# A fused feed-forward, attention, feed-forward block: new rope, projections, root mean square and order of units in the attention stage

## The reference

```
x = x + 0.5 * ffn(layernorm(x))        # mixture of 8 experts, 2 chosen
x = x + attention(layernorm(x))
x = x + 0.5 * ffn(layernorm(x))
```

```
q, k, v = x Wq^T + bq, x Wk^T + bk, x Wv^T + bv
q1, q2, k1, k2 = rope(each)                    # (x1 cos - x2 sin, x1 sin + x2 cos)
a1, a2 = softmax(causal(q1 k1^T / sqrt 8)), softmax(causal(q2 k2^T / sqrt 8))
out = (a1 - lam a2) v                          # lam per head, from lq1, lk1, lq2, lk2
out = out * rsqrt(mean(out*out over 8) + 1e-6) * head_norm_w * 0.8
result = out Wo^T + bo
```

## Time and profile before

| | |
|---|---|
| median of three runs | 1861.6 us |
| profiled execution | 1863.29 us |
| its span, first to last instruction | 1861.6 us |
| mean granted TensorE clock | 0.968 of full speed |
| PE busy | 1608.8 us, 86% |
| DVE busy | 1363.2 us, 73% |
| ACT busy | 1269.4 us, 68% |
| POOL busy | 1046.3 us, 56% |

### The profile page before, as it was taken

The page is one execution under the profiler, slowest core; times in us unless marked ns, Lnnn a source line. Parts: engine busy times, 40 slices in busy tenths (PEclk is TensorE's granted clock), DMA queues, the critical chain, the costliest instruction groups (busy, mean ns, idle before and its releaser), DMA issues. The chain is left out here.

```text
span 1861.6 us, 43161 instructions
## 1 busy us (share of the span) xinstructions
PE 1608.8 (86%) x16448; PEld 1220.1 (66%) x16448; DVE 1363.2 (73%) x3442; ACT 1269.4 (68%) x1613; POOL 1046.3 (56%) x707
## 2 busy tenths in 40 slices
PE   4999999994588888888888888888873799999998
PEld 3787777883466666666666666666652577778787
DVE  5777777765778778878887788788742677777775
ACT  4777777772167767767677677677664577777776
POOL 4888888875324434334344343343312688888885
PEclk9999999997699999999999999999996799999999
DMA  3333323321323233232232332322302232233331
GB/s 113 103 114 115 102 88 108 109 103 46 87 79 92 58 91 82 66 94 72 76 94 61 86 87 60 95 78 70 89 12 77 97 115 90 93 114 110 108 109 63
DMA packets 142846, 163.14 MB, mean 88 GB/s; under 512 B 13244, under 2 KB 124558, under 8 KB 141454
## 3 DMA queue, kind: packets, MB, share of 16 engines
q1 hardware_dynamic: 142640, 160.38, 28.8%
HBM read 91.20 MB, written 14.70 MB: 57 GB/s over the span
## 5 line engine op out<-in xcount | busy, mean ns | idle before, releaser
L292 POOL TENSOR_TENSOR ffn_h_low<-ffn_h,ffn_h_high 128x1024 fp32r<-128x1024 f32 x192 | 458.4, 2401 | 95.0 <-ACT ffn_h_high L341 94.8
L1019 ACT ACTIVATE att_prob<-att_ring 128x1024 f32<-128x1024 f32 x384 | 388.6, 1022 | 155.9 <-PE att_ring L1240 153.4
L1125 DVE TENSOR_REDUCE att_nmax<-att_ring 128x4 f32<-128x1024 f32 (+1 forms) x384 | 450.8, 1217 | 54.3 <-PE att_ring L1240 54.3
L479 DVE TENSOR_TENSOR ffn_h<-ffn_up,ffn_comb_wide 128x1024 f32<-128x1024 f32 x256 | 311.3, 1216 | 125.1 <-ACT ffn_up L334 122.8
L334 ACT ACTIVATE ffn_up<-ffn_up 128x1024 f32<-128x1024 f32 x256 | 258.1, 1008 | 202.8 <-PE ffn_up L567 201.1
L341 ACT ACTIVATE ffn_h_high<-ffn_h 128x1024 fp32r<-128x1024 f32 x256 | 269.3, 1052 | 0.7 <-DVE ffn_h L479 0.7
L935 POOL TENSOR_TENSOR att_qk<-att_turned 128x512 f32<-128x512 f32 x64 | 81.4, 1273 | 318.0 <-DVE att_turned L1104 318.0
L1240 PE MATMUL att_ring<-att_qs,att_kd 64*128 64x256 bf16 (+1 forms) x2048 | 151.1, 249 | 95.4 <-DVE att_nmax L1125 57.2
L567 PE MATMUL ffn_up<-ffn_xt_high,ffn_w_high 128*128 128x512 f32 x512 | 214.7, 419 | 1.7 <-DVE ffn_h L479 1.6
L580 PE MATMUL ffn_y<-ffn_h_high,ffn_w_high 128*128 128x512 f32 x512 | 205.3, 401 | 7.0 <-POOL ffn_h_low L292 6.0
L284 POOL TENSOR_TENSOR ffn_ez<-ffn_e_const,ffn_nz 128x16 f32<-128x16 f32 x64 | 185.6, 2901 | 38.2 <-DVE ffn_nz L405 38.2
(11 more groups left out here) (146 smaller groups left out, 2840.7 us busy)
## 6 DMA issues: line engine op xcount, KB each, us to landing
ffn_comb_wide<-ffn_comb_d SPq DMA_DIRECT2D x128, 512.0 KB, 5.6
att_qs<-att_parts SPq DMA_DIRECT2D x192, 128.0 KB, 2.5
att_kd<-att_parts SPq DMA_DIRECT2D x192, 128.0 KB, 2.5
ffn_x<-x SPq DMA_DIRECT2D x32, 256.0 KB, 3.1
ffn_w<-w SPq DMA_DIRECT2D x4, 1024.0 KB, 7.2
x<-ffn_out SPq DMA_DIRECT2D x16, 256.0 KB, 2.4
att_x<-x SPq DMA_DIRECT2D x32, 128.0 KB, 2.3
att_xr<-x SPq DMA_DIRECT2D x32, 128.0 KB, 2.3
```

The costliest lines, as they stand in the source:

```text
L292: nc.gpsimd.tensor_tensor(hts[1][:, e % NH], h[:, e % NH], hts[0][:, e % NH], ALU.subtract).then_inc(low_by_pool, 1)
L479: nc.vector.tensor_tensor(h[:, e % NH], up[:, e % NUP], comb_wide[:, b.c % NW, e].unsqueeze(1).to_broadcast([P, HE, FT]), ALU.mult).then_i ...
L1019: nc.scalar.activation(prob[:, u % NP], ring[:, ORDER.index((kind, u)) % 3], ACT.Exp, scale=SCALE).then_inc(prob_ready, 1)
L1125: nc.vector.tensor_reduce(nmax[:, b, :, h0:h0 + cnt], ring[:, pos % 3] .rearrange("p (s h k) -> p s h k", s=2, k=width), AX.X, ALU.max, ne ...
```

## The change

1. Rope. The bias is taken out of the product with cosine and sine: one DVE multiplication of 128x1024 replaces four of 128x256 in each QK unit, and POOL adds a rotated bias, computed once at the start (`biased`), in a second addition in "rotate".
2. Projections. QK and V no longer multiply in fp32 but as three fp32r products each (`PRODUCTS`: high x high, high x low, low x high) with the weights and the transposed input split in two; the weights are split at the start, the input's low part `xts[1]` by a DVE subtraction after XT.
3. Mean squares. The inverse root is one power on POOL over 32 columns ("rms"); Ln, Exp and the Newton step are gone.
4. Maxima. NM transposes `nmax` in fp32. ACT copies the high part, DVE subtracts it ("max left"), ACT copies the middle part ("max mid"), POOL subtracts the low part ("max low"), and SP then writes them out in another layout.
5. Normalising is done by ACT, as x * rstd + shift; DVE computes the shift of two columns ("shift").
6. `ORDER` and `AFTER` are new. In the new order the first units are XT, NM, S0, QK0, T6, QK1, so S0 now stands ahead of QK0; OT, V and OP stand at the end.

```diff
-ORDER = [("XT", 0), ("T", 6), ("QK", 0), ("NM", 0), ("QK", 1), ("S", 0), ("S", 1), ("T", 7), ("T", 8), ("S", 2),
-         ("S", 3), ("T", 9), ("S", 4), ("T", 10), ("S", 5), ("T", 11), ("S", 6), ("S", 7), ("T", 0), ("V", 0),
-         ("T", 1), ("T", 2), ("NT", 0), ("NT", 1), ("OT", 0), ("S", 8), ("OP", 0), ("S", 9), ("T", 3), ("S", 10),
-         ("T", 4), ("S", 11), ("T", 5)]
+ORDER = [("XT", 0), ("NM", 0), ("S", 0), ("QK", 0), ("T", 6), ("QK", 1), ("T", 7), ("S", 1), ("T", 8), ("S", 2),
+         ("S", 3), ("S", 4), ("T", 9), ("S", 5), ("T", 10), ("S", 6), ("S", 7), ("T", 11), ("T", 0), ("S", 8),
+         ("T", 1), ("S", 9), ("T", 2), ("S", 10), ("T", 3), ("NT", 0), ("T", 4), ("NT", 1), ("T", 5), ("S", 11),
+         ("OT", 0), ("V", 0), ("OP", 0)]
 
 AFTER = {
-    "rotate 0": ("T", 6), "rotate 1": ("T", 7),
-    "left 0": ("T", 8), "left 1": ("T", 9), "low 0": ("T", 10), "low 1": ("T", 0),
-    "high 0": ("QK", 1), "high 1": ("T", 8), "mid 0": ("T", 9), "mid 1": ("T", 10),
-    "weigh 0": ("T", 5), "weigh 1": ("T", 7), "weigh 2": ("T", 11), "weigh 3": ("T", 0),
-    "copy 0": ("T", 5), "copy 1": ("T", 7), "copy 2": ("T", 11), "copy 3": ("T", 0),
-    "streams": ("T", 4), "ms": ("XT", 0), "rms": ("T", 6), "newton": ("S", 1), "scaled": ("T", 0),
-    "stats": ("S", 7), "rstd": ("S", 8), "normalise": ("S", 10),
+    "rotate 0": ("QK", 1), "rotate 1": ("T", 9), "left 0": ("S", 4), "left 1": ("T", 9), "low 0": ("S", 7),
+    "low 1": ("S", 9), "high 0": ("S", 4), "high 1": ("S", 6), "mid 0": ("T", 9), "mid 1": ("T", 2),
+    "weigh 0": ("S", 11), "weigh 1": ("XT", 0), "weigh 2": ("S", 4), "weigh 3": ("T", 1), "copy 0": ("V", 0),
+    "copy 1": ("T", 8), "copy 2": ("S", 8), "copy 3": ("T", 1), "streams": ("T", 2), "ms": ("XT", 0),
+    "rms": ("XT", 0), "scaled": ("S", 9), "stats": ("T", 0), "rstd": ("T", 1), "shift": ("S", 8),
+    "max left": ("NM", 0), "max mid": ("S", 0), "max low": ("T", 8), "normalise": ("T", 3),
 }
...
-                        nc.gpsimd.tensor_tensor(qk[:, n], turned[:, n, 0], turned[:, n, 1], ALU.add).then_inc(qk_ready, 1)
+                        nc.gpsimd.tensor_tensor(qk[:, n], turned[:, n, 0], turned[:, n, 1], ALU.add).then_inc(rotated, 1)
+                        wait(pool, rotated, turn.at(1, 2, n + 1))
+                        nc.gpsimd.tensor_tensor(qk[:, n], qk[:, n], biased[:, n].rearrange("p c q -> p (c q)"),
+                                                ALU.add).then_inc(qk_ready, 1)
...
+                def rms(turn):
+
+                    wait(pool, norm_step, turn.at(-3, NORM, NORM))
+
+                    wait(pool, pool_norm, turn.at(-4, 5, 3))
+                    nc.gpsimd.tensor_tensor(rrms[:], ms_eps[:], minus_halves[:], ALU.pow).then_inc(rrms_ready, 1)
...
-                            nc.scalar.activation(nmax_t[:], ring[0:2 * 3 * H, ORDER.index((kind, u)) % 3, 0:S // 2]
-                                                 .bitcast(BF16), ACT.Copy).then_inc(read["NM"], 1)
+                            nc.scalar.activation(nmax_t[:, 0], ring[0:HS, ORDER.index((kind, u)) % 3, 0:S],
+                                                 ACT.Copy).then_inc(max_high, 1)
+                        if (kind, u) == AFTER["max mid"] and turn.runs(-1):
+                            wait(act, read["NM"], turn.at(-1, 1, 1))
+                            nc.scalar.activation(nmax_t[:, 1], nmax_left[:], ACT.Copy).then_inc(max_mid, 1)
+
+                def normalise(turn):
+                    wait(act, shift_ready, turn.at(2, 1, 1))
+
+                    wait(act, pe["XT"], turn.at(1, 1, 1))
+                    for t in range(QB):
+                        last = nc.scalar.activation(xn[:, t], x[:, turn.slot(2), t], ACT.Identity, bias=shift[:, t:t + 1],
+                                                    scale=rstd[:, t:t + 1])
+                    last.then_inc(xn_ready, 1)
...
+                            nc.vector.tensor_tensor(turned[:, u].rearrange("p n (c q) -> p n c q", c=2),
+                                                    ring[:, pos % 3].rearrange("p (n c q) -> p n c q", n=2, c=2),
+                                                    rope[:].unsqueeze(2).to_broadcast([P, 2, 2, S]),
+                                                    ALU.mult).then_inc(read["QK"], 1)
...
-                                wait(te, read["XT"], turn.at(1, 1, 1))
+                                wait(te, xt_low, turn.at(1, 1, 1))
                                 for n in range(4):
-                                    last = mm(buf[:, n * S:(n + 1) * S], wqk[:, 4 * u + n], xt[:])
+                                    for i, (a1, a2) in enumerate(PRODUCTS):
+                                        last = mm(buf[:, n * S:(n + 1) * S], wqks[a1][:, 4 * u + n], xts[a2][:],
+                                                  start=(i == 0), stop=(i == 2))
```

More of the change, by code:

```diff
@@ L739, in attention @@
         rstd = sb("rstd", [P, QB])
+        shift = sb("shift", [P, QB])
         xn = sb("xn", [P, QB, D])
-        xt = sb("xt", [P, S])
+        wqks = [sb(f"wqk_{n}", [P, 2 * NC4, P], F32R) for n in ("high", "low")]
+        wvs = [sb(f"wv_{n}", [P, D], F32R) for n in ("high", "low")]
+        xts = [sb(f"xt_{n}", [P, S], F32R) for n in ("high", "low")]
         turned = sb("turned", [P, 2, 2, 2 * S])
         qk = sb("qk", [P, 2, 2 * S])
+        biased = sb("biased", [P, 2, 2, S])
         left = sb("left", [P, 2, 2 * S])
@@ L984, in body @@
                                     low_part(turn, n, what)
+                        if (kind, u) == AFTER["rms"] and turn.runs(-3):
+                            rms(turn)
                         if (kind, u) == AFTER["scaled"] and turn.runs(-3):
                             scaled(turn)
+                        if (kind, u) == AFTER["max low"] and turn.runs(-1):
+                            wait(pool, max_mid, turn.at(-1, 1, 1))
+                            nc.gpsimd.tensor_tensor(nmax_t[:, 2], nmax_left[:], nmax_t[:, 1], ALU.subtract).then_inc(max_low, 1)
                         if (kind, u) == AFTER["streams"] and turn.runs(-2):
@@ L1033, in body @@
                                 o_copy(turn, GROUP_OFFSET[g], g)
-                        if (kind, u) == AFTER["rms"] and turn.runs(-3):
-                            wait(act, norm_step, turn.at(-3, NORM, 7))
-                            nc.scalar.activation(ln_ms[:], ms_eps[:], ACT.Ln).then_inc(rms_step, 1)
-                            wait(act, rms_step, turn.at(-3, 2, 1))
-                            nc.scalar.activation(y0[:], ln_ms[:], ACT.Exp, scale=-0.5).then_inc(rms_step, 1)
                         if kind == "OT" and turn.runs(-3):
@@ L1044, in body @@
                                                  ACT.Copy).then_inc(read["OT"], 1)
+                        if (kind, u) == AFTER["normalise"] and turn.runs(2):
+                            normalise(turn)
                         if kind == "NM" and turn.runs(-1):
@@ L1180, in clear_keys @@
+                        if (kind, u) == AFTER["max left"] and turn.runs(-1):
+                            wait(dve, max_high, turn.at(-1, 1, 1))
+                            wait(dve, max_low, turn.at(-2, 1, 1))
+                            nc.vector.tensor_tensor(nmax_left[:], ring[0:HS, ORDER.index(("NM", 0)) % 3, 0:S], nmax_t[:, 0],
+                                                    ALU.subtract).then_inc(read["NM"], 1)
                 def clear_keys(k):
@@ L1231, in free @@
                         back -= 3
-                    if kind == "T":
+                    if kind == "XT":
+                        wait(te, xt_low, before.at(1, 1, 1))
+                    elif kind == "T":
                         wait(te, prob_ready, before.at(offset(kind, u), 12, u + 1))
```

134 lines of the change are left out of this document (68 added, 66 removed).

## The result

The changed kernel takes 1848.93 us, the median of five runs (1842.10 to 1849.69), against 1861.72 for the kernel before; the ratio is 0.9919, 95% interval 0.9899 to 0.9938. It is faster, by 12.8 us where the prediction had 51. The profiled execution has a span of 1847.2 us against 1861.6.

A forecast was written before the change was run, and what follows sets the result against it. The prediction took attention to be bound by a ring of three PSUM buffers, with no engine full. Thirty turns x 1.93 = 58 us, less 7 outside them, gave 51 off 1861.6: 1811 us, range 1788 to 1850.

The forecast's parts named there:

- The ring of three buffers: Attention turn: TensorE computes into PSUM, VectorE or ScalarE reads, buffer returns; walked at 26.6 us a turn, down from 28.53.
- The power: Inverse root of the mean squares on GpSimd over 128x32: 5.4 us, at most 5.8.
- the product: VectorE's rope multiplication of 128x1024 from PSUM, one per QK unit: near 1216 ns.
- the projections' spacing: TensorE's fp32r products of 256 columns 0.126 us apart, so a QK unit of 12 takes 1.5 us.
- POOL's 19.5 us: GpSimd's work per attention turn grows from 11.19 to 19.5 us and still fits.
- the absence of table loads: ScalarE in attention: Exp is the only table function left, so no load of 1283 ns in a steady turn.
- The loop through rotation, split and DMAs: From one S0 through projections, rope, split and twelve DMAs to the next: 24.7 to 26.1 us, just under 26.6.
- Rival A: The loop from S0 to S0 paces attention: turn 27.2 to 28 us, 1847 us at 27.8; chance 0.22.
- Rival E: Table loads stay on ScalarE, 2.57 us a turn, about +1 a turn, 1841 us; counted inside Rival A's chance.
- it costs at most 0.5, within the handoff allowance: Maxima's rows, read back by DMA, arrive at about 14.3 us after XT where T0 wants them at 13.75.
- 4+2.3+1.4+3-3.3 is +7: Outside steady turns: set-up, added adds, end power and drain wait, less start-up savings; between +2 and +12 us.
- VectorE's saving: VectorE's work per attention turn falls by 2.2 us of 23.08.

The follow-up runs named there:

- e4: Changed kernel with new places on GpSimd and ScalarE only: max low first, rotations and splits moved forward, the power after S9; 1816.73 us, ratio 0.9758.
- e2: Changed kernel with only the place of "max low" moved on GpSimd, ahead of the first rotation; 1830.04 us, ratio 0.9828.
- e5: On e4: set-up rearranged, ScalarE normalises the first row before splitting weights, TensorE waits for split weights only at the first QK unit; 1817.28 us.
- e6: On e4: QK0 and S0 swapped in TensorE's order, so QK0 comes before S0 again; 1825.91 us, ratio 0.9806.
- e10: On e4: normalising put back on VectorE, two operations after T3 in place of the shift; 1822.61 us, ratio 0.9793.
- e8: Changed kernel with Ln and Exp on ScalarE and the Newton step on VectorE back in place of GpSimd's power, new order kept; 1903.43 us, ratio 1.0218.
- e3: Changed kernel with the projections back in fp32 and no low part of XT on VectorE; 1852.42 us, ratio 0.9942.

## Why the prediction was wrong

The steps inside the turn held. The ring of three buffers walked through the new order gave 26.6, and the chip 26.84, or 26.67 with POOL's order mended (e4). The power, the product, the projections' spacing, POOL's 19.5 us and the absence of table loads came as worked out. The loop through rotation, split and DMAs was under the turn as walked: in the window from 600 to 1300 no unit waits for the twelve DMAs. Rival A (the loop paces, 1847) gave nearly the measured time by another mechanism, and its sign, idle TensorE before S0 on a DMA, isn't there. So it is luck that 1848.93 lies within 1788 to 1850. Rival E is refuted by the one table load. Against the rule of the Trainium skill (TensorE: Matmul & The Clock Gate, section "The mechanism"), by which a QK unit would take 2.6 us, products 0.12 apart with a full-row load each show loads hidden under products. (The same section also names a background weight buffer, into which a load may go ahead; the prediction left that out.)

Of the 36.6 us (rounded below) by which the span's gain fell short (51 against 14.4):

- **18.5 us: "it costs at most 0.5, within the handoff allowance".** This is the step that failed. The rows' path was walked with one landing time, and T0 left without slack. The median landing was right; but 13 of 32 landings are 0.6 to 1.8 us later, by the fetches shown above, and TensorE stands. A wait of 1.61 us made that turn 2.48 us longer: 1.03 by the wait, less the 0.58 that the ring takes back, and some 1.45 by the lower clock that follows. In 928.86 to 932.20 the granted clock is 0.53 of full, the lower of its two levels (1.2 GHz) for nearly all of it; in the 2.00 us before, TensorE had been busy for 0.39. The prediction also names this wait as the sign to look for ("TensorE idle before T0 would mean that the maxima come later than walked"), and gave it no price and no rival. e2 shows that 19 us come back when the rows are sent earlier.
- **6.5 us: the turn of 26.84 for 26.6**, 27 turns. 4.6 of it is the places of the steps on POOL and ACT (e4: 26.67).
- **about 12 us: "4+2.3+1.4+3-3.3 is +7".** By turn 3 the kernel after is 9.25 us behind the kernel before (559.02 against 549.77), of which 5.3 are there at the first XT, and at the end 3.6 are lost (545.0 against 541.4 from the last XT to the end of the span). 12.9 in all; the prediction's +7 less three turns of 1.93 allowed 1.2. The part that was mis-sized is the fill, and less so the end: the first S0 waits for a chain that the ring doesn't cover yet. The kernel before has no wait of TensorE for a DMA there.

```profile
480.98 0.61 PE L1277 MATMUL att_ring<-att_kd,att_qs 64*128 64x128 bf16 x8 [6.14 <-DMA att_kd<-att_parts]
505.89 0.61 PE L1277 MATMUL att_ring<-att_kd,att_qs 64*128 64x128 bf16 x8 [1.69 <-DMA att_kd<-att_parts]
```

The set-up on DVE was sized well as work (4 to 5 us), but e5 shows that taking it off the first XT brings nothing in the end. What counts in the fill is the latency of the key chain: S0 ahead of QK0 costs 1.9 us there (e6), and with rotations and splits put in front turn 3 begins 5.5 us earlier (e4). The power has no part in that, as the first one starts at 560.3, after turn 3 began.

VectorE's saving was over-estimated (0.5 against 2.2), for 1.3 us by the two operations beside GpSimd, which the prediction took as unchanged. It didn't matter, as e10 shows for 0.5 us more: an engine at 22.6 of 26.8 us is not the bound, the holding of buffers is.

## What to carry to other kernels

A deadline that is met with no slack by the median landing of a DMA is missed whenever the landing is late; read the spread (the longest, not the median) from the trace of before, even where no one waits for it there, and give the path at least that much, here 1.8 us (3.32 against 1.57 in the kernel before). In a ring of buffers price the order of units and the order within each engine first: here all the cheaper instructions in the old order were worth 0.36 us a turn and the new order on top of them 1.33, and moving one 0.66 us instruction on POOL was worth 19 us. The two don't add up by themselves: the new order without the power was slower than the old (e8). Fill and drain are chains of latency, and an order that pays in the steady turn can cost there (e6: S0 ahead of QK0 gains 0.21 us a turn and costs 1.9 in the fill).

## What the runs showed of the hardware

- A 16 KB fetch of instructions that begins within 1.0 us after a 48 KB write was issued (or 0.2 before) puts off the write's landing: the dependent reads are issued 1.9 to 3.5 us after it instead of 1.6, in all of 81 cases. Period and phase follow TensorE's instruction stream.
- The landing is not the only cost of a stall: after five of twelve waits of 1.0 to 2.2 us TensorE ran 3.4 us at its lower clock, which made the turn 1.4 to 1.6 us longer.
- A VectorE product of 128x32 takes 0.19 us with GpSimd idle and 0.63 when it starts while a GpSimd instruction of 128x256 still has most of its way to go. Beside the power it stays at 0.19 (e4).
- GpSimd's power takes 5.44 us for 128x32, on the line through 0.71 (2 columns) and 2.90 (16).
- fp32r products of 256 columns with a 128x128 load each follow one another every 0.12 us; three of them replace one fp32 product and a unit is 0.3 us shorter for it (1.61 against the 1.93 of e3).
